# A graph attention layer on one core: products ten steps behind the scores instead of eleven, with x's bank stages, value groups and queue orders moved to match

## The reference: what is computed

```
h     = relu(layernorm(x))
att_n = tanh(neigh @ Wn1 + bn1) @ Wn2 + bn2        # 4096 x 32
value = neigh @ Wv + bv                            # 4096 x 128
att_x = tanh(h @ Wx1 + bx1) @ Wx2 + bx2            # 4096 x 32
ws    = leaky_relu(att_x @ att_n.T, 0.01)          # 4096 x 4096
ws    = softmax(where(adj > 0, ws, -9e15), axis=1)
out   = x + concatenate([h @ Wfx + bfx, ws @ value], axis=1)
```

## Time and profile before

| | |
|---|---|
| median of three runs | 485.35 us |
| the profiled execution, its own time | 485.15 us |
| its span in the trace | 482.8 us |
| PE busy | 464.3 us (96%) |
| PE weight loads | 424.5 us (88%) |
| DVE busy | 427.7 us (89%) |
| ACT busy | 428.3 us (89%) |
| POOL busy | 258.4 us (54%) |
| granted TensorE clock, mean | 0.998 of full |

### The profile page before, as it was taken

One profiled execution on the slowest core, in us unless ns is written; L12 is line 12 of the kernel. 1 busy time (PEld: TensorE's weight loads), 2 busy tenths in 40 slices (PEclk: granted clock), 3 DMA queues, 4 the chain that ended last, 5 costly groups with the idle time before them and its releaser, 6 DMA issues.

```text
span 482.8 us, 10844 instructions
## 1 busy us (share of the span) xinstructions
PE 464.3 (96%) x3728; PEld 424.5 (88%) x3728; DVE 427.7 (89%) x820; ACT 428.3 (89%) x714; POOL 258.4 (54%) x361
## 2 busy tenths in 40 slices
PE   8997789999999999999999999999999999999997
PEld 7975579998899899998999899999899899999896
DVE  3678899999999899989999999989999899999764
ACT  2464899999999999999999999999999999999973
POOL 3108247853677547945686557845686455454300
PEclk9999999999999999999999999999999999999999
DMA  8944635457555655557456654657457554553000
GB/s 303 304 88 90 153 67 89 81 90 163 106 88 93 130 118 100 100 90 157 93 88 109 131 110 91 109 99 159 79 95 139 91 88 79 108 100 56 11 12 12
DMA packets 32373, 51.51 MB, mean 107 GB/s; under 512 B 2368, under 2 KB 22976, under 8 KB 32320
## 3 DMA queue, kind: packets, MB, share of 16 engines
q0 software_dynamic: 9216, 33.56, 42.5%
q1 hardware_dynamic: 22816, 17.17, 11.0%
q10 hardware_dynamic: 288, 0.10, 0.2%
HBM read 80.19 MB, written 4.19 MB: 175 GB/s over the span
## 4 chain that ended last, share of the span: by engine, by line
PE 75%; ACT 5%; issue 3%; DVE 3%; POOLq 0%; POOL 0%; DVEq 0%; ACTq 0%
PE ps_turned L922 20%; PE ps_product L943 11%; PE ps_product L945 11%; PE ps_product L944 11%; PE ps_scores L900 10%; PE ps_scores L899 6%; PE ps_product L865 3%; ACT scores L561 3%; ACT pt_hi L523 2%; DVE scores L706 2%; PE ps_product L857 1%; PE ps_product L841 1%; ACT scores L549 1%; PE ps_product L848 1%; PE ps_product L954 1%
## 5 line engine op out<-in xcount | busy, mean ns | idle before, releaser
L453 POOL TENSOR_TENSOR scores<-scores,mask 128x512 f32<-128x512 f32 x117 | 136.4, 1166 | 116.9 <-ACT scores L549 116.3
L688 DVE TENSOR_TENSOR pt_lo<-ps_turned,pt_hi 128x512 fp32r<-128x512 f32 x256 | 173.9, 685 | 20.8 <-PE ps_product L945 9.8
L523 ACT ACTIVATE pt_hi<-ps_turned 128x512 fp32r<-128x512 f32 x256 | 158.1, 618 | 20.9 <-PE ps_turned L922 20.3
L943 PE MATMUL ps_product<-pt_hi,v_hi 128*128 128x256 f32 x512 | 164.9, 322 | 0.1
L922 PE MATMUL ps_turned<-ident,scores 128*128 128x128 f32 x1024 | 153.8, 273 | 0.8 <-DVE pt_lo L688 0.6
L561 ACT ACTIVATE scores<-scores,low_top 128x1024 f32<-128x1024 f32 x128 | 151.5, 1183 | 0.0
L945 PE MATMUL ps_product<-pt_lo,v_hi 128*128 128x256 f32 x512 | 144.5, 282 | 0.0
L944 PE MATMUL ps_product<-pt_hi,v_lo 128*128 128x256 f32 x512 | 144.0, 281 | 0.0
L549 ACT ACTIVATE scores<-ps_scores 128x1024 f32<-128x1024 f32 x128 | 133.3, 1041 | 9.6 <-PE ps_scores L900 9.4
L922 PEld LDWEIGHTS ps_turned<-ident,scores 128*128 128x128 f32 x1024 | 121.9, 140 | 17.7 <-issue 2.0
L706 DVE CUSTOM_DVE_ANT_0 scores<-ps_scores,scores,low_top 128x1024 f32<-128x1024 f32 x96 | 122.5, 1276 | 0.9 <-ACT scores L549 0.4
(11 more groups left out here) (70 smaller groups left out, 359.8 us busy)
## 6 DMA issues: line engine op xcount, KB each, us to landing
adj_in<-in_adj POOLq DMA_DIRECT2D x60, 512.0 KB, 5.4
scores<-in_neigh_t SPq DMA_DIRECT2D x8, 512.0 KB, 7.9
x_rows<-in_x SPq DMA_DIRECT2D x7, 512.0 KB, 5.9
x_left<-in_x SPq DMA_DIRECT2D x8, 256.0 KB, 5.7
x_right<-in_x SPq DMA_DIRECT2D x16, 128.0 KB, 5.3
scores<-in_adj POOLq DMA_DIRECT2D x4, 512.0 KB, 6.4
out_h<-x_left SPq DMA_DIRECT2D x8, 256.0 KB, 2.3
out_h<-x_right SPq DMA_DIRECT2D x16, 128.0 KB, 2.1
```

Source lines behind the costliest of these rows:

```text
L453: pool.tensor_tensor(half, half, mask[:, s % MASK_RING, BANK:CHUNK], ALU.add).then_inc(masked, 1)
L523: act.activation(pt_hi[:, (2 * b + u) % HI_RING], pt[:, u], ACT.Copy).then_inc(hi_done, 1)
L688: dve.tensor_tensor(pt_lo[:, u], pt[:, u], pt_hi[:, (2 * b + u) % HI_RING].bitcast(FP32), ALU.subtract).then_inc(lo_done, 1)
L943: pe.matmul(product_of(g), v_hi[:, block, :], high, start=block == 0, stop=False)
```

## The change

- Turns and products run ten steps behind the scores, not eleven (`BACK_LAG`). POOL's masks begin one step sooner with it.
- x's stages are moved in the bank: PE's two turns from steps 6 and 8 to 5 and 7, first layer and tanh from 10 to 8, second layer from 14 to 13, the left output from 15, 17, 19, 19 to 14, 15, 16, 17. DVE's statistics go from 10, 10, 10, 12 to 8, 9, 10, 12 and their join from 14 to 12.
- Five value groups instead of four are made in the neighbour phase, the other three one step sooner.
- ACT's list is reordered: `power` and `rise` first, then `hi(s, 0)`, x's work, `aggregate`, `hi(s, 1)`.
- PE does x's work before `turn(s, 1)` instead of after it, and DVE the rest of the neighbours last but for the mask.

```
-BACK_LAG = ASTEPS + 3
+BACK_LAG = ASTEPS + 2
-X_LOAD = -12
-X_STATS = (-6, -6, -6, -4)
-X_AGGR = -2
-X_RSTD = (-2, -2, -1, 0)
-X_NORM = (1, 3, 3, 4)
-X_TURN = (6, 8)
-X_FIRST, X_TANH = 10, 10
+X_LOAD = -10
+X_STATS = (-8, -7, -6, -4)
+X_AGGR = -4
+X_RSTD = (-4, -3, -1, 0)
+X_NORM = (1, 2, 3, 3)
+X_TURN = (5, 7)
+X_FIRST, X_TANH = 8, 8
...
-V_START, V_STRIDE = 2, 2
+V_START, V_STRIDE = 1, 2
 LEFT_0 = 5
-AHEAD_STATS = 0
-WIDE_0 = 1
-V_FRONT, V_LAG = 4, 1
+AHEAD_STATS = -1
+WIDE_0 = 4
+V_FRONT, V_LAG = 5, 1
...
@@ the list of ACT @@
             def step(s):
+                power(s)
+                rise(s)
                 hi(s, 0)
+                side(s)
                 aggregate(s)
-                rise(s)
                 hi(s, 1)
-                side(s)
-                power(s)
...
@@ the list of DVE @@
                 lo(s, 0)
                 close(s)
-                neigh_rest(s)
                 x_work(s)
                 lo(s, 1)
+                neigh_rest(s)
...
```

More of the change, by code:

```diff
@@ L75 @@
 END = STEPS + FIN_LAG - ASTEPS + 2
-X_LOAD = -12
-X_STATS = (-6, -6, -6, -4)
-X_AGGR = -2
-X_RSTD = (-2, -2, -1, 0)
-X_NORM = (1, 3, 3, 4)
-X_TURN = (6, 8)
-X_FIRST, X_TANH = 10, 10
[L85 to L89, removed]
-V_START, V_STRIDE = 2, 2
+X_LOAD = -10
[5 more added lines that the diff above has]
+X_FIRST, X_TANH = 8, 8
+X_SECOND = (13, 13)
+X_STACK = (13, 13)
+X_WIDE, X_LEFT = (14, 15, 16, 17), 17
+X_LEFT_LOAD, X_SUM = 10, (11, 12)
+X_RIGHT = 5
+V_START, V_STRIDE = 1, 2
 LEFT_0 = 5
-AHEAD_STATS = 0
-WIDE_0 = 1
-V_FRONT, V_LAG = 4, 1
+AHEAD_STATS = -1
+WIDE_0 = 4
+V_FRONT, V_LAG = 5, 1
 POOL_MASKS = BACK_LAG
```

## The result

| | before | after |
|---|---|---|
| median, runs beside each other | 485.1 us (484.67 to 485.37, 8 runs) | 482.06 us (481.35 to 483.92, 8 runs) |
| ratio, with its 95% interval | | 0.9942 [0.9928, 0.9956] |
| the profiled execution, its own time | 485.15 us | 481.35 us |
| its span | 482.8 us | 479.4 us |

The change makes the kernel 0.6% faster: 3.0 us by the medians, 3.8 by the profiled executions (3.4 by their spans). The forecast was 481.7. The total came out, but two of its three terms did not, and they cancel.

The account below looks back on a forecast made before the run. The prediction took PE to bound the main loop, with little room in ACT and DVE. Its terms, -5.7 + 2.5 - 0.4 = -3.6 us, took the profiled 485.15 to 481.55, median 481.7 us; range 478.5 to 487.0.

Parts of the forecast that it names:

- What bounds the kernel: Main loop: PE binds, busy 49.60 of 50 us; ACT (47.91) and DVE (47.30) have little room behind it.
- The rival in which ACT takes PE's place: Main loop: ACT's 3.00 us step equals PE's, so half of term 1 is lost, 484.5 us; chance 0.17.
- Term 1: Main loop: the exponential at the head of ACT's step ends the leak's wait, 0.80 us per bank, -5.7 us.
- Term 2: Main loop: DVE waits for x's rows in each bank, PE stalls 0.5 us in five banks, +2.5 us.
- L: Main loop: time from issue to landing of the load of x's rows, taken as 5.2 us.
- statistics that don't wait: Main loop: sign against the forecast, which expected waits for the rows' load of about 1.2 us, six or so.
- The rival of rows in time: Main loop: rows land within 4.7 us, so only the gains are left, 479.2 us; chance 0.20.
- Term 3: Before the main loop: six terms of either sign sum to -0.4 us, bounded by -1.5 and +2.
- one fewer step: Before the main loop: one step fewer than eleven before the first turn, at 2.7 us each, gives -2.7 us.
- the wait of step 9: Before the main loop: the 1.87 us that step 9's leak waits for the exponential goes, -1.9 us.
- the value rest: Before the main loop: a value rest leaves DVE's steps, -0.6 us.
- the value layer of step 1: Before the main loop: step 1's value layer now waits for DVE's last attention rest, +0.4 us.

Follow-up runs that it names:

- The kernel with both orders: Kernel before, with ACT's list in the new order and PE's work for x ahead of its second turn, eleven steps kept: 479.95 us, 0.9895.
- a wait made on purpose: Changed kernel with the first statistics of x's rows in step -9 instead of -8, one step nearer to their load: 495.94 us, 1.0211.
- POOL's two sums in a later place: Changed kernel with x's wide layer back in step 1 and POOL's two right sums in steps 6 and 7, not ahead of the steps: 480.3 us, 0.9894.
- a kernel whose mask was held: Changed kernel with the wide layer of x back in step 1 instead of step 4 (WIDE_0 = 1): 483.81 us, 0.9967.

## Why the prediction came out, point by point

**What bounds the kernel: right.** PE binds in the loop, ACT has time to spare (it waited 15.1 us for the turns in the kernel after, 20.3 before), and PE's own work gives 3.00 in a plain step. The rival in which ACT takes PE's place is out: PE is busy 50.00 of 50.

**Term 1: right in place and size, incomplete in cause.** Forecast -5.7, measured 5.42 + 0.32 = 5.74. The wait of the earlier trace rows went, and the first copy is what is late next, without harm, as the text had it. But the forecast ascribed all to ACT's list. That list alone gave 0.13 us per bank. It pays only with PE's work for x ahead of the second turn, since it puts ACT's work for x ahead of a copy; the two together gave 0.81. I counted PE's edit at nothing and never asked what ACT's moved `side` would wait for. The stretched masks, for which the prediction let 0.13 us per bank stay, went too (longest 0.65 us). The kernel with both orders still has masks of 1.5 us in the loop and takes 52.83 us for a bank, only 0.10 more, so they cost little.

**Term 2: the step that failed is L.** Forecast +2.5, measured 0: PE has no gap in the loop. The condition (PE stalls by the lateness beyond what it has in hand) was tried by a wait made on purpose and held, 2.1 us for each where 2.2 were expected. Two inputs were off. L was taken as 5.2, between the least and the middle of the earlier trace rows; it was 4.0. And DVE comes 4.47 us after the issue, not 4.04 (4.06 by the prediction's own terms), since ACT's copies are later. The prediction had itself named statistics that don't wait as a sign that it is wrong.

The reason given for a shorter L, the load's distance from the adjacency loads, fits: they now go out at 104.61 and 110.99 with the rows' load at 108.32 between them, where it followed one by 1.1 us. In the kernel before, the one load that followed an adjacency load by 4.7 us took 4.6, the five that followed by 1.1 took 5.7 to 6.9. The adjacency load behind the rows' load doesn't seem to count: with the wait made on purpose it came 5.4 us or more after it, not 2.7, and the median was 4.2. In all eleven kernels with the load in step 7 of the bank its median was 3.7 to 4.2 us, in the three with it in step 8 it was 5.8 to 6.0. What besides the distance counts (the store and x's other loads also lie otherwise) wasn't tried.

The fit that the prediction quotes from the Trainium skill, DMA: Bandwidth & Descriptors, Anatomy of one DMA, is given there for DMAs that GpSimd issues, and the rows' load is issued by SyncE; its 3.2 us, an estimate, was nearer to the 4.0 than the 5.2 of the sum, and still below the least of 3.8. The rival of rows in time had the true mechanism, at a total that was too low.

**Term 3: the step that failed is one fewer step.** Forecast -0.4, measured +2.3: +2.7 before the loop and -0.4 in the tail (the profiled execution's earlier start hides another 0.7 of the loss). The fifth value group was priced rightly, +1.9 against 1.75 and 1.79. But -2.7 for one step fewer, -1.9 for the wait of step 9 and -0.6 for the value rest assumed that each would reach the end. The ten steps took 30.75 us, where the prediction's terms make 29.34 - 2.7 - 0.6 - 1.9 + 1.8 + 0.4 = 26.3: 4.4 too few. Step 0 and the steps from 10 to 16 came 0.8 and 0.5 better than the terms, the tail 0.4. The 0.4 for the value layer of step 1 was far off as well: step 1 took 7.58 us where it had taken 4.21.

The experiments show why a sum of single waits fails here. Taking away 4.2 us of PE's wait in step 1 gave nothing by step 10, and taking away the rows' wait of 1.85 gave 0.1 by step 16. The wait of step 9 can be followed in the kernel with both orders and eleven steps: there it is gone and step 10 comes 1.6 us earlier after step 0, but step 16 only 0.2 (46.06 against 46.26). DVE, ACT, PE and POOL wait for each other in turn. The most by step 16, 4.0 us (52.97 to 48.94 after step 0), came with POOL's two sums in a later place, against a kernel whose mask was held; against the changed kernel it is 1.7 (50.66). Why the ten steps lost 3.0 us in the changed kernel is known in part: at most 0.3 by step 10 is the lower clock. Its mask took 0.86, less than the 1.02 that the same mask took before, so that isn't it. The rest stays open; that moving POOL's list helped most makes it the first place to look.

**The sum.** -5.7 + 0 + 2.3 = -3.4 us is the difference of the spans, against the -3.6 of the forecast. The errors of -2.5 and +2.7 cancel. That two terms failed by the same amount in opposite directions is luck; only term 1 came out by what it describes.

## What to carry to other kernels

When one engine's list is reordered, ask for each item moved forward what it waits for, and whether that producer's list has it in time; two lists are one edit. A transfer's time depended here on what was issued ahead of it, so when a load moves between others, its old durations bound it badly. In a start-up phase in which no engine is full, price a wait by an experiment and not by its length: 4.2 us taken away were worth nothing.

## What was not expected of the hardware

- **A VectorE operation can be held for as long as GpSimd works beside it.** The mask of 0.42 us took 2.92 and 2.85 beside four additions of 0.7 us in two kernels; beside the same four it took 0.86 in the changed kernel and 0.94 in another, and 0.95 beside two. In the short cases the second addition took 0.89 or 0.90 us instead of 0.72, in the long ones none was longer. The Trainium skill, SBUF — State Buffer, SBUF: two separate sides, says that the two engines share a pair of ports under a lock, held for a whole instruction by the one that starts first, if the VectorE operation is in a 2-port mode or has two inputs in SBUF; no run here shows in which mode the mask is. The traces agree with such a lock: the mask came in behind the first addition, or behind all four. What decides between the two they don't tell: it started 0.14 us after the first addition both when it took 0.86 and when it took 2.92.
- **The clock fell after a wait of PE and cost little.** After 4.64 us without work the granted clock was at the level of 1.2 GHz from 40 to 43 us (0.50), and half a value group took 2.08 us for 1.05. Kept full, it gave at most 0.7 us by step 16.
- **The same load of 512 KB took 4.0 or 5.9 us** at the median, in the changed kernel and in the one before. It was issued 3.7 and 1.1 us behind the last adjacency load; that this alone decides is not shown.
